# Weight tiles of the FP4 feed-forward dealt over the attention sweeps by a table instead of one per head pair

## The chip, the cores and the metric

The kernel runs on the 8 cores of one Trainium2 chip, each core on one batch element (4096 tokens of 1024 channels) with the same program and no exchange between cores. The metric is the device time in microseconds (us) of the slowest core.

## The reference

Per batch element, with x of 4096x1024:

```python
xn = layernorm(x)
# causal attention, 16 heads of 64, one shared k and v head, then an output layernorm
q = layernorm(xn) @ w_q.T ; k, v = split(layernorm(xn) @ w_kv.T)
s = layernorm(softmax(causal(q k^T)) v @ w_out.T)
# FP4 feed-forward: blocks of 16 along the contracted axis, grid 0 .5 1 1.5 2 3 4 6
def fp4_linear(x, w): return fp4_quant_dequant(x) @ fp4_quant_dequant(w).T
h = silu(fp4_linear(xn, w_gate)) * fp4_linear(xn, w_up)    # w_gate, w_up: 2816x1024
g = silu(fp4_linear(h, w_down))                            # w_down: 1024x2816
out = x + s * g
```

All three feed-forward weights have to be quantized and transposed before the feed-forward begins. That is 52 tiles of 128 rows: 22 of w_gate and 22 of w_up with 1024 columns (short tiles), and 8 of w_down with 2816 columns (long tiles).

## The kernel before

The kernel has three stages. `emit_w` transposes the attention weights. `emit_a` (L586) does the attention, the preparation of x and, in between, the 52 weight tiles. `emit_f` does the feed-forward from DRAM copies of the quantized, transposed weights, behind a barrier on everything before it.

`emit_a` has nine turns of `sup` (0 to 8). Turn 0 prepares four row tiles of x. Each turn from 1 to 8 runs `emit_sweeps(sup - 1)`: 512 queries against 4·sup key tiles, for eight head pairs `w` (0 to 7). After it come the output projection with its layernorm, and `emit_qhat` for the next 512 queries. I call one head pair of one turn a slot; there are 64. A slot of turn `sup` has 4·sup keys: for each key TensorE writes scores to `ps_a` or `ps_b`, ScalarE takes the exponential into `expb`, TensorE accumulates in `ps_o`. At the end ScalarE copies `ps_o` to `aosb`, forms the reciprocal row sums `rb`, sends them through DRAM (`dsw_d`, back as `dtsw`), and VectorE multiplies them in (`AOn`, L547).

Ahead of the sweep of slot w a closure `inject[w]` (L635) emits other work. In turns 1 to 7 it prepares the four next row tiles of x: `p0_ve_part` (L320, layernorm, quantization and a second layernorm on VectorE, with two small ScalarE instructions in each `ln_apply`) in w0 to w3, and `p0_pe_part` (L338, transposes, key and value projections) one slot later, in w1 to w4. Then, in every slot, it emits the weight work:

- `w_tile_pe` (L296) for the tile pending from the slot before: for each 128 columns a TensorE transpose of `wcast` into `ps_o` and a VectorE copy to `xqTst`, in groups of up to eight, each group followed by a store issued from ScalarE's queue. A group waits (L301) until the store before has landed.
- `w_tile_ve` (L282) for the next tile: its load to `wtile` on SyncE's queue, which waits until the tile before is quantized, and `quant` on VectorE, in pieces of 1024 columns, into `wcast`. The tile becomes pending.

So each slot takes one tile. The tiles are used up in order: turns 1 to 5 have the first 40 short tiles, turn 6 has the last four short ones in w0 to w3 and long ones in w4 to w7, turn 7 has long ones in w0 to w3 with the last transposes in w4, and turn 8 has none. The `while` loop at L642 would take what is left, and finds nothing.

Every engine runs its instructions in the order in which this program emits them. A wait in `transpose_chunks` (L194) stands in TensorE's own stream, ahead of the score matmuls of the slot, and the copies stand in VectorE's stream behind `AOn` of the slot before:

```python
        pe.wait(ve, pe_gate_ve)          # L194: the quantized tile
        ...
            npt = pe.op("transpose", tgt[:, 0:128], src_ap[:, sl(ch)],
                        s["identb"][:])
            ve.wait(pe, npt)
            self._tr_free[ch % 2] = ve.op("tensor_copy", dst_fn(ch),
```

`wcast` has two buffers, `wtile` one, the staging buffer of `xqTst` for weights one.

Of the kernel before, what the change touches and what calls it, by code (L numbers as in the profile page):

```python
# [78 lines left out]
class Builder:  # L79
# [506 lines left out]
    def emit_a(self):  # L586
        pe, ve, ac, po, ld, stq = (self.pe, self.ve, self.ac, self.po,
                                   self.ld, self.stq)
        s, st_ = self.s, self.streams
        NSUP = self.NSUP  # L590

        ve.wait_dma(st_["Lmisc"], self._n_greps)
        ve.wait_dma(st_["Swsp"], st_["Swsp"].n)
        self.xt_free = [0, 0]
        self.xst_free = [0, 0]
        self.sst_free = [0, 0]
        self._vtr_free = 0
        self._k2_evac = 0
        self._k2r_ac = 0
        self._op_free_ve = 0  # L600
        self._xqt_pe = [0, 0]
        self._xnlt_pe = [0, 0]
        self._pe_after_sweeps = 0
        self._preA_ve = 0
        self._ao_free = (ve, 0)
        self.aosb_free_ve = [0, 0]
        self.nmd = 0
        self.nmq = 0
        self.n_k2 = 0

        for sup in range(NSUP + 1):
            if sup == 0:
                for t in range(4):
                    nx = self.p0_ve_part(t)
                    self.p0_pe_part(t, nx)
            if sup >= 1:
                base = 4 * sup
                nx_hold = {}

                def mk_both(ttv, ttp, _b=base, _h=nx_hold, _last=(sup == NSUP)):  # L620
                    def f():
                        if not _last:
                            if ttv is not None:
                                _h[ttv] = self.p0_ve_part(_b + ttv)
                            if ttp is not None:
                                self.p0_pe_part(_b + ttp, _h[ttp])
                        if self._w_pend is not None:
                            self._w_tile_pe(self._w_pend)
                            self._w_pend = None
                        if self.wffn_parts:  # L630
                            self._w_pend = self._w_tile_ve(
                                *self.wffn_parts.pop(0))
                    return f

                inject = [mk_both(0, None), mk_both(1, 0),  # L635
                          mk_both(2, 1), mk_both(3, 2),
                          mk_both(None, 3), mk_both(None, None),
                          mk_both(None, None), mk_both(None, None)]
                self.emit_sweeps(sup - 1, inject)
            if sup < NSUP:  # L640
                self.emit_qhat(sup)
        while self.wffn_parts or self._w_pend is not None:  # L642
            if self._w_pend is not None:
                self._w_tile_pe(self._w_pend)
                self._w_pend = None
            if self.wffn_parts:
                self._w_pend = self._w_tile_ve(*self.wffn_parts.pop(0))
# [340 lines left out]
```

How the kernel before makes its waits and increments, by code:

```python
    def wait(self, other, val):  # L35
        if val > 0:
            self.e.wait_ge(other.sem, val)
# [1 line left out]
    def wait_dma(self, dmaq, n):  # L39
        if n > 0:
            self.e.wait_ge(dmaq.sem, 16 * n)
# [1 line left out]
    def op(self, name, *a, **k):  # L43
        if self.serialize and self.n > 0:
            self.e.wait_ge(self.sem, self.n)
        r = getattr(self.e, name)(*a, **k)
        r.then_inc(self.sem, 1)
        self.n += 1
        return self.n
# [7 lines left out]
    def wait(self, other, val):  # L57
        if val > 0:
            self.e.wait_ge(other.sem, val)
# [1 line left out]
    def wait_dma(self, stream, n):  # L61
        if n > 0:
            self.e.wait_ge(stream.sem, 16 * n)
# [9 lines left out]
    def dma(self, out, in_, **k):  # L73
        self.q.e.dma_start(out=out, in_=in_, **k).then_inc(self.sem, 16)
        self.n += 1
        return self.n
# [572 lines left out]
    def emit_f(self):  # L649
# [147 lines left out]
                po.op("tensor_tensor", s["t0f"][:], s["t0f"][:], s["g_sb"][:],  # L797
                      ALU.mult)
                sld_free[fb] = po.n
                po.wait_dma(st_["So%d" % fb], o_free[fb])
                no = po.op("tensor_tensor", s["o_sb"][:, fb, :], s["t0f"][:],
                           s["xr"][:, fb, :], ALU.add)
                xr_free[fb] = no
                stq.wait(po, no)
                o_free[fb] = st_["So%d" % fb].dma(g["out_d"][sl(gt), :],
                                                  s["o_sb"][:, fb, :])
        self.nc.sync.wait_ge(st_["So0"].sem, 16 * st_["So0"].n)
        self.nc.sync.wait_ge(st_["So1"].sem, 16 * st_["So1"].n)
```

## Time and profile before

| | |
|---|---|
| median of 2 runs | 7600.37 us (7597.98 to 7602.76) |
| profiled execution | 7599.55 us, span of its slowest core 7598.0 us |
| spans of the 8 cores | 7546.9 to 7598.0 us |
| busy on the slowest core | DVE 55%, PE 48%, ACT 25% |
| attention stage | to about 4970 us, the feed-forward from there |

PE is TensorE's matmuls, DVE is VectorE, ACT is ScalarE, SP is SyncE. A "q" behind an engine's name is its own instruction stream, from which DMAs are issued. The clock is TensorE's granted clock as a share of 2.4 GHz. All times in the trace are microseconds from the start of the span of core 4, the slowest. Every instruction has the line of the helper that issues it (L46), so groups are told apart by the tiles that they write and read.

### The profile page before, as it was taken

The numbers are of one execution on the slowest core, as the hardware profiler recorded it, in microseconds if no ns is written. First come the engines' busy times: TensorE is split into PE (matmuls) and PEld (weight loads), VectorE is DVE, ScalarE is ACT, GpSimd is POOL, SyncE is SP. The second block draws the span as 40 slices with busy tenths as digits, with TensorE's granted clock in tenths as the row PEclk, the third lists the DMA queues.
The fourth block names the chain that finished last, engine by engine and source line by source line (L and its number), as shares of the span: only waits on it lengthen the run. The fifth ranks groups of instructions, "written<-read, shape, count | busy, mean of one in ns | idle before, by whom it ended". The sixth has DMA issues, their size and how long they took to land.

```text
span 7598.0 us, 56896 instructions; the slowest of 8 cores (7546.9 to 7598.0 us)
## 1 busy us (share of the span) xinstructions
PE 3646.3 (48%) x12721; PEld 1345.8 (18%) x12952; DVE 4146.2 (55%) x6907; ACT 1905.8 (25%) x2394; POOL 194.7 (3%) x119
## 2 busy tenths in 40 slices
PE   2224243344354455435444657644565565546556
PEld 1011011111111111111111212211221122122112
DVE  5575663653553543447477110058838846883883
ACT  0112222232242343334232637601101100100110
POOL 0000000000000000000000000000020010002002
PEclk9756566666666677667666879867777777768777
DMA  2011010110100000011001000020020002002001
GB/s 72 17 32 31 27 36 21 32 32 16 31 25 21 24 27 23 19 32 36 24 31 36 17 9 12 13 79 23 14 81 23 25 31 61 23 14 80 26 22 47
DMA packets 210741, 236.14 MB, mean 31 GB/s; under 512 B 110696, under 2 KB 159976, under 8 KB 209256
## 3 DMA queue, kind: packets, MB, share of 16 engines
q1 hardware_dynamic: 88992, 164.78, 6.9%
q10 hardware_dynamic: 121424, 67.72, 3.1%
q8 instruction: 120, 1.97, 0.1%
q14 instruction: 205, 1.68, 0.1%
HBM read 164.76 MB, written 67.70 MB: 31 GB/s over the span
## 4 chain that ended last, share of the span: by engine, by line
DVE 43%; PE 23%; ACT 12%; issue 11%; DMA 7%; DVEq 2%; ACTq 1%; SPq 1%; POOL 0%; POOLq 0%
DVE f_qs_c L46 16%; PE ps_o L46 14%; DVE qs_c L46 8%; PE ps_a L46 6%; ACT expb L46 6%; PE ps_b L46 3%; DVE f_qs_m L46 3%; DVE t0f L46 2%; DVE bn L46 2%; DVE hq L46 2%; DVE hsb L46 2%; DMA dsw_d<-rb 2%; DMA dtsw<-dsw_d 2%; DVEq L45 1%; DVE qs_m L46 1%
## 5 line engine op out<-in xcount | busy, mean ns | idle before, releaser
L46 PE MATMUL ps_o<-expb,VhX 128*128 128x512 bf16 x2213 | 744.9, 417 | 314.8 <-ACT expb L46 278.7
L46 PE MATMUL ps_a<-wgb,xqT_S 128*128 128x512 bf16 (+1 forms) x1475 | 742.8, 504 | 101.3 <-DMA wub<-wquT_s 77.0
L46 ACT ACTIVATE expb<-ps_a 128x1024 bf16<-128x1024 f32 x576 | 589.3, 1023 | 798.2 <-PE ps_a L46 714.9
L46 PE MATMUL ps_b<-wub,xqT_S 128*128 128x512 bf16 (+1 forms) x1536 | 761.1, 496 | 10.3 <-issue 5.3
L46 DVE TENSOR_TENSOR AOn<-aosb,dtsw 64x512 bf16<-64x512 f32 x128 | 87.9, 686 | 1149.9 <-DMA dtsw<-dsw_d 1142.6
L46 DVE SCALAR_TENSOR_TENSOR f_qs_c<-f_qs_aa,f_qs_c 128x512 f32<-128x512 f32 (+1 forms) x960 | 621.6, 648 | 104.1 <-DVE f_qs_c L46 5.5
L46 DVE SCALAR_TENSOR_TENSOR qs_c<-qs_aa,qs_c 128x1024 f32<-128x1024 f32 (+1 forms) x500 | 601.8, 1204 | 53.1 <-DVE qs_c L46 1.4
L46 ACT ACTIVATE expb<-ps_b 128x1024 bf16<-128x1024 f32 x576 | 589.3, 1023 | 152.1 <-PE ps_b L46 122.7
L46 PE MATMUL ps_a<-identb,hq 128*128 128x128 bf16 x704 | 104.8, 298 | 1037.4 <-DVE hq L46 1037.4
L46 PE MATMUL ps_o<-identb,xq_t 128*128 128x128 bf16 x256 | 60.1, 255 | 1072.4 <-DVE xqTst L46 953.6
L46 PE MATMUL ps_o<-identb,wcast 128*128 128x128 bf16 x664 | 169.2, 264 | 685.4 <-DVE xqTst L46 414.0
L46 PE MATMUL ps_a<-QT,KT 65*128 65x512 bf16 x1152 | 433.2, 444 | 33.3 <-DMA QT<-mrow_d 31.8
L46 PE MATMUL ps_b<-QT,KT 65*128 65x512 bf16 x1152 | 420.0, 432 | 0.7 <-issue 0.4
L46 ACT ACTIVATE lnv<-st,epsT 128x1 f32<-128x1 f32 x96 | 28.3, 294 | 1413.6 <-DVE st L46 1413.6
L46 PE MATMUL ps_o<-wqd_sb,hqT 128*128 128x512 bf16 x1376 | 350.2, 417 | 45.8 <-ACT g_sb L46 38.4
L46 ACT ACTIVATE hqT<-ps_a 128x512 bf16<-128x512 bf16 (+1 forms) x192 | 107.8, 561 | 1025.8 <-PE ps_a L46 1025.8
L46 DVE TENSOR_TENSOR hsb<-hg,ps_b 128x512 f32<-128x512 f32 (+1 forms) x192 | 123.4, 643 | 411.3 <-ACT hg L46 391.8
L46 ACT ACTIVATE hg<-ps_a 128x512 f32<-128x512 f32 (+1 forms) x192 | 107.8, 561 | 932.5 <-PE ps_b L46 702.0
L46 PE MATMUL ps_o<-w_oT,AOn 128*128 128x512 bf16 x502 | 195.0, 570 | 275.2 <-DVE st_s L46 171.7
L46 PEld LDWEIGHTS ps_o<-expb,VhX 128*128 128x128 bf16 x2304 | 173.0, 101 | 846.3 <-issue 833.2
L46 DVE COPY xqTst<-ps_o 128x128 bf16<-128x128 bf16 x784 | 176.0, 224 | 183.3 <-PE ps_o L46 88.6
L46 PEld LDWEIGHTS ps_a<-wgb,xqT_S 128*128 128x128 bf16 x1536 | 199.5, 130 | 414.8 <-issue 358.8
(107 smaller groups left out, 4767.0 us busy)
## 6 DMA issues: line engine op xcount, KB each, us to landing
wgb<-wqgT_s SPq DMA_DIRECT2D x20, 1024.0 KB, 6.0
wub<-wquT_s SPq DMA_DIRECT2D x20, 1024.0 KB, 8.4
x_t<-L_attn_x SPq DMA_DIRECT2D x32, 512.0 KB, 4.5
dsw_d<-rb ACTq DMA_DIRECT2D x128, 128.0 KB, 2.4
dtsw<-dsw_d SPq DMA_DIRECT2D x128, 128.0 KB, 2.6
xr<-L_attn_x SPq DMA_DIRECT2D x32, 512.0 KB, 4.9
out<-o_sb ACTq DMA_DIRECT2D x32, 512.0 KB, 4.9
wtile<-L_ffn_w_gate SPq DMA_DIRECT2D x22, 512.0 KB, 4.2
```

The lines of the kernel that those rows point to most:

```text
L45: self.e.wait_ge(self.sem, self.n)
L46: r = getattr(self.e, name)(*a, **k)
```

## The change

A table `wq` says how many weight tiles a turn takes, and `nsl` spreads them over its eight slots; the weight part of the closure is repeated so often. With eight sweeps the table is: turns 1 to 4 none, turn 5 one tile per slot (8), turn 6 two per slot (16), turn 7 two per slot (16), turn 8 twelve, in the slots w0 to w7 as 1, 2, 1, 2, 1, 2, 1, 2. That is 52. The x preparation stays where it was. In a slot with two tiles the order of emission is: transposes and copies of the pending tile, load and quantization of a first tile, transposes and copies of that first tile, load and quantization of a second tile, which is then pending. In a turn with no tiles the loop body of the weight part doesn't run, so nothing pending is handled either. The 52nd tile is pending when turn 8 ends, and its transposes fall to the `while` loop at L642.

In order, turns 5 to 7 and the first four tiles of turn 8 are the short tiles (40 and 4), and the last eight of turn 8 (from the first tile of w3 on) are the long ones.

```diff
             if sup >= 1:
                 base = 4 * sup
                 nx_hold = {}
+                wq = {NSUP - 3: 8, NSUP - 2: 16,
+                      NSUP - 1: 16, NSUP: 12}.get(sup, 0) if NSUP >= 4 else 7
 
-                def mk_both(ttv, ttp, _b=base, _h=nx_hold, _last=(sup == NSUP)):
+                def mk_both(ttv, ttp, nw, _b=base, _h=nx_hold,
+                            _last=(sup == NSUP)):
                     def f():
                         if not _last:
                             if ttv is not None:
                                 _h[ttv] = self.p0_ve_part(_b + ttv)
                             if ttp is not None:
                                 self.p0_pe_part(_b + ttp, _h[ttp])
-                        if self._w_pend is not None:
-                            self._w_tile_pe(self._w_pend)
-                            self._w_pend = None
-                        if self.wffn_parts:
-                            self._w_pend = self._w_tile_ve(
-                                *self.wffn_parts.pop(0))
+                        for _ in range(nw):
+                            if self._w_pend is not None:
+                                self._w_tile_pe(self._w_pend)
+                                self._w_pend = None
+                            if self.wffn_parts:
+                                self._w_pend = self._w_tile_ve(
+                                    *self.wffn_parts.pop(0))
                     return f
 
-                inject = [mk_both(0, None), mk_both(1, 0),
-                          mk_both(2, 1), mk_both(3, 2),
-                          mk_both(None, 3), mk_both(None, None),
-                          mk_both(None, None), mk_both(None, None)]
+                def nsl(i):
+                    return wq * (i + 1) // 8 - wq * i // 8
+
+                inject = [mk_both(0, None, nsl(0)), mk_both(1, 0, nsl(1)),
+                          mk_both(2, 1, nsl(2)), mk_both(3, 2, nsl(3)),
+                          mk_both(None, 3, nsl(4)), mk_both(None, None, nsl(5)),
+                          mk_both(None, None, nsl(6)),
+                          mk_both(None, None, nsl(7))]
                 self.emit_sweeps(sup - 1, inject)
```

## Rows read from the trace of the kernel before

**Rows 1.** The page: its first line, and the chain that ended last, by engine.
```profile
span 7598.0 us, 56896 instructions; the slowest of 8 cores (7546.9 to 7598.0 us)
...
DVE 43%; PE 23%; ACT 12%; issue 11%; DMA 7%; DVEq 2%; ACTq 1%; SPq 1%; POOL 0%; POOLq 0%
```

**Rows 2.** Waits of PE: engine tile <- releaser: us in total, times, longest us.
```profile
PE ps_o L46 <- DVE xqTst L46: 1375.6, 347, 41.2
...
PE ps_o L46 <- DVE wcast L46: 128.6, 26, 15.9
```

**Rows 3.** Timeline of turn 1, w5 to w6: start us, us, what, [idle before <- releaser].
```profile
608.62 1.29 ACT L46 ACTIVATE aosb<-ps_o 128x512 f32<-128x512 f32 x2 [1.30 <-PE ps_o L46]
...
617.03 0.39 PE L46 MATMUL ps_o<-identb,wcast 128*128 128x128 bf16 x2 [8.98 <-DVE wcast L46]
618.59 1.48 DVE L46 TENSOR_TENSOR AOn<-aosb,dtsw 64x512 bf16<-64x512 f32 x2 [1.81 <-DMA dtsw<-dsw_d]
620.17 0.55 DVE L46 COPY xqTst<-ps_o 128x128 bf16<-128x128 bf16 x2
...
622.62 0.59 PE L46 MATMUL ps_a<-QT,KT 65*128 65x512 bf16 x1
...
623.26 1.22 DVE L46 TENSOR_REDUCE qs_m<-wtile 128x64 f32<-128x1024 f32 x1
...
639.05 1.23 DVE L46 TENSOR_TENSOR wcast<-qs_c,qs_d 128x1024 bf16<-128x1024 f32 x1
```

**Rows 4.** Windows: stretch, us, busy of PE, PEld, DVE, ACT, POOL, clock, DMA, GB/s.
```profile
4228.20:4267.00 38.80, 32.79 (x120) 10.89 (x123) 0.31 (x2) 28.64 (x28) 0.00 (x0) 0.90 0.02 6
...
4309.00:4351.40 42.40, 32.22 (x120) 10.68 (x121) 1.37 (x2) 31.71 (x34) 0.00 (x0) 0.88 0.05 13
...
4571.30:4901.90 330.60, 251.84 (x932) 82.90 (x949) 9.61 (x14) 250.67 (x259) 0.00 (x0) 0.91 0.04 12
```

**Rows 5.** Timeline of ACT, turn 7, w4 to w5 (no tile in w5).
```profile
4267.03 1.29 ACT L46 ACTIVATE aosb<-ps_o 128x512 f32<-128x512 f32 x2 [1.00 <-PE ps_a L46]
...
4271.94 1.02 ACT L46 ACTIVATE expb<-ps_a 128x1024 bf16<-128x1024 f32 x1 [1.46 <-issue]
...
4275.28 1.02 ACT L46 ACTIVATE expb<-ps_a 128x1024 bf16<-128x1024 f32 x1 [1.21 <-PE ps_a L46]
4276.99 1.02 ACT L46 ACTIVATE expb<-ps_b 128x1024 bf16<-128x1024 f32 x1 [0.68 <-PE ps_b L46]
```

**Rows 6.** Timeline of PE in the same stretch.
```profile
4273.21 1.01 PE L46 MATMUL ps_o<-expb,VhX 128*128 128x512 bf16 x2 [5.58 <-ACT expb L46]
```

**Rows 7.** Timeline of turn 5, w1 to w2, with x preparation and one short tile.
```profile
2601.99 1.48 DVE L46 TENSOR_TENSOR AOn<-aosb,dtsw 64x512 bf16<-64x512 f32 x2 [23.00 <-DMA dtsw<-dsw_d]
...
2641.16 0.27 PE L46 MATMUL ps_o<-identb,wcast 128*128 128x128 bf16 x1
...
2644.50 1.01 PE L46 MATMUL ps_a<-QT,KT 65*128 65x512 bf16 x2
```

**Rows 8.** Timeline of turn 2, w0.
```profile
814.76 0.20 ACT L46 ACTIVATE rstd<-lnv 128x1 f32<-128x1 f32 x1
...
822.60 1.02 ACT L46 ACTIVATE expb<-ps_a 128x1024 bf16<-128x1024 f32 x1 [7.63 <-PE ps_a L46]
```

**Rows 9.** Timelines of DVE, ACT and PE, turn 6, w5 to w6, with long tiles.
```profile
3483.11 0.55 DVE L46 COPY xqTst<-ps_o 128x128 bf16<-128x128 bf16 x2
...
3498.01 1.22 DVE L46 TENSOR_REDUCE qs_m<-wtile 128x64 f32<-128x1024 f32 x1
...
3546.18 1.48 DVE L46 TENSOR_TENSOR AOn<-aosb,dtsw 64x512 bf16<-64x512 f32 x2
...
3561.49 1.01 PE L46 MATMUL ps_a<-QT,KT 65*128 65x512 bf16 x2
...
3531.44 1.29 ACT L46 ACTIVATE aosb<-ps_o 128x512 f32<-128x512 f32 x2 [1.00 <-PE ps_o L46]
```

**Rows 10.** DMA issues: out<-in, queue, count, KB each, median us to landing.
```profile
wtile<-L_ffn_w_down SPq DMA_DIRECT2D x8, 1408.0 KB, 6.3
```

## The prediction

> **What bounds the kernel now.** I read the page first. The chain that ended last is DVE for 43% and PE for 23% [rows 1], so it changes hands, and an average says little. The list of PE's waits shows where they meet: PE stood 1375.6 us for copies of transposed tiles (`xqTst`) and 128.6 us for a quantized weight tile (`wcast`) [rows 2]. To see what a slot (one head pair of one turn) pays I then read three kinds of it in the timeline, and their lengths in the windows.
>
> A slot with one short tile and no x preparation [rows 3]: the sweep ends at 608.62 (`aosb`). The tile was quantized before 617.03, but its copies stand on DVE behind `AOn`, which waits for the round trip of the row sums through DRAM and starts at 618.59. The copies run from 620.17, PE reaches the next scores at 622.62, 14.0 us after `aosb`; over the 15 such slots of turns 1 to 5 this gap is 14.0 to 15.3, mean 14.4. Then DVE quantizes the next tile from 623.26 to 640.28 (17.0 us) beside the sweep. Note what sets the 14 us: the round trip (10.0) and `AOn` (1.6), and only the last 3.1 us are the copies. The quantization costs nothing, it lies under sweep and round trip. Coupling PE to DVE is the price, and it is paid once per slot, whatever is quantized beside the sweep.
>
> A slot with no tile [rows 5]: from `aosb` at 4267.03 to the next exponential at 4271.94, 4.9 us, because PE emits the next scores at once and `AOn` is nobody's business. In lengths at 28 keys [rows 4]: 38.8 from first score to `aosb`, plus 14.4 is 53.2 with a tile; 42.4, 42.0 and 42.1 without (the first stands in the rows). **A coupled slot costs 11.0 us more than a free one.** In turn 8 the seven slots w1 to w7 are free, 330.6/7 = 47.2 us each [rows 4].
>
> A slot with x preparation (w1 to w3; w4 has its TensorE half) is coupled anyway: `AOn` at 2601.99, then the preparation on DVE and its own copies; the weight tile's transposes begin only at 2641.16 and the scores at 2644.50 [rows 7]. So there a short tile costs 3.3 us.
>
> **The change, part by part.** Five prices are needed.
>
> 1. A coupling added or taken away: 11.0 us.
> 2. A short tile's copies in a slot that is coupled anyway: 3.3 us.
> 3. A second short tile in a slot. Its transposes wait for its own quantization, and they stand in PE's stream ahead of the sweep. Nothing lies beside it: DVE comes from the pending tile's copies, PE and ACT have nothing else before the scores. 17.1 us of quantization (pitch from one piece of 1024 to the next; the single one above was 17.0), 0.6 us until the first transposed pair is ready to copy (an estimate: two transposes of 0.27 [rows 7]), 3.1 us of copies (620.17 to 623.26 [rows 3]): 20.8 us. The trace never shows a tile quantized and transposed in one slot, so this sum has bounds: not below 17.0 + 3.1 = 20.1, since both are DVE's own work in order, and not above 20.8 plus a load that comes late. The load of the first tile waits for nothing in that slot (the pending tile was quantized in the slot before). The load of the second tile waits for the first's quantization and has the copies to hide in, and what is left lies under the sweep. I take 20.8.
> 4. A second long tile: its quantization takes 3498.01 to 3546.18, 48.2 us, its copies with the two waits for staging stores 3483.11 to 3498.01, 14.9 us [rows 9]. With 0.5 us of start, 63.6. Its load lands 6.3 us after issue [rows 10], and it is issued behind the `dtsw` loads, some 8 us after `aosb`, where DVE wants it 14.4 us after: nothing, or 2 us in one slot.
> 5. A long pending tile instead of a short one: 14.9 - 3.1 = 11.8 us. In turn 6 the long quantization also outlasted the sweep: `aosb` 3531.44, `AOn` 3546.18, 14.7 instead of 10, scores at 3561.49, a gap of 30.0 [rows 9]. In turn 8, 43.9 us of sweep and 10.1 of round trip cover 48.2.
>
> Also w0: there PE isn't held by x preparation (nothing precedes), but ACT is, by the second `rstd` of `ln_apply`, which stands in ACT's stream ahead of the exponentials. In turn 2 it ends at 814.96, and the first exponential runs at 822.60, after the tile's copies and the scores [rows 8]. Without a pending tile the scores are ready long before, and the exponential would start some 0.1 us behind the `rstd`: 7.5 us gained, in turns 2 to 5.
>
> Gains:
> - turn 1: w1 to w4 4 x 3.3, w5 to w7 3 x 11.0: 46.2
> - turns 2 to 4: the same and 7.5 for w0, 53.7 each: 161.1
> - turn 5: w0 only, since it still has a tile per slot: 7.5
>
> Together 214.8 us.
>
> Losses:
> - turn 6 (was: short in w0 to w3, long quantized from w4): w0 to w4 5 x 20.8 = 104.0. w5 to w7: gap 14.4 + 20.8 = 35.2 instead of about 30.1: 3 x 5.1 = 15.3. Sum 119.3.
> - turn 7 (was: long pending in w0 to w4, w5 to w7 free): w0 20.8 - 11.8, less 5.3 for an `AOn` of turn 6 that is no longer late: 3.7. w1 to w4: 4 x (20.8 - 11.8) = 36.0. w5 to w7: 3 x (11.0 + 20.8) = 95.4. Sum 135.1.
> - turn 8 (was free): w0 has one pending short tile behind the wait for `QT` (L463 stands ahead of `inject`), 3.3. w1: 31.8. w2: 11.0. w3, a second long tile behind a short pending one: 11.0 + 63.6 = 74.6. w4, one long pending: 22.8. w5: 22.8 + 63.6 = 86.4. w6: 22.8. w7: 86.4. Sum 339.1.
> - the tail: the last long tile's transposes after the last output projection, with nothing beside them and the feed-forward's barrier behind: 14.9, and 0.6 for a store that lands later than the last of `s_s`. 15.5.
>
> Together 609.0 us. Net **+394.2 us**. The feed-forward isn't touched.
>
> The profiled execution took 7599.55 us (span 7598.0), 0.8 us under the median of the runs. 7599.6 + 394.2 = 7993.8, so I say 7994 us, 5.2% longer.
>
> One place where the clock could move the gains. With a tile, PE comes to each sweep out of a long idle time; a free sweep too finds PE idle, since it waits 5.58 us for the first exponential and its first pair of matmuls takes 1.01 us [rows 6], the same as the first scores of a coupled one (1.01 [rows 7]). The clock over a whole sweep of 28 keys is 0.90 coupled and 0.88 free [rows 4]. So I let free and coupled sweeps cost the same per key. The Trainium skill (TensorE: Matmul & The Clock Gate, "HAM oscillation — how this bites in real kernels") says that waits between bursts of matmuls drop the clock to half again and again, and that a loop that keeps PE busy keeps it up. By that rule the 12 freed sweeps of turns 1 to 4 would open at the full clock and save the 1.21 + 0.68 = 1.9 us for which ACT waits on slow scores at a sweep's start [rows 5], some 22 us more gain, and the sum would be 372 instead of 394. The rows speak against it: that wait stands in a free sweep.
>
> **The rivals.**
>
> *A, the forecast:* the second tile holds PE. 7994 us. Chance 0.86.
>
> *B, the other side: the second tile's work is hidden.* DVE idles some 23 us in a slot before `AOn` ([rows 7], "23.00 <-DMA dtsw<-dsw_d"), so there is room, and it would take DVE running the quantization there. The change adds 17 first short tiles and 3 long ones. If all of their price vanished, 17 x 20.8 + 3 x 63.6 = 544.4 us go from the sum: 7449 us, 2.0% faster. If only quantization vanished and the copies stayed, 435 us go: 7559 us, no change. It turns to faster by over 2% only where 546 us or more vanish. Against it: in the order of emission the first tile's quantization comes behind the pending tile's copies, these behind `AOn`, and the wait of PE's transposes is ahead of the scores. Chances: 0.01 for faster, 0.03 for no change.
>
> *C: the early turns give back little.* If freed slots of 4 to 16 keys were still paced by the round trip of the row sums (`aosb` waits for the `dsw_d` store before, and this for the `dtsw` load before that), only the 3.1 us of copies would go in those 12 slots: 12 x 7.9 = 95 us less gain, 8089 us. For it: the trace has no free slot under 28 keys. Against: the round trip of 10 us fits into the shortest free slot, which is 4.9 + 4 x 1.7 = 11.7 us at the slow opening pace of 1.71 us per key [rows 5]. Chance 0.05.
>
> *D: the late sweeps slow down.* If after 35 to 90 us of idle time PE stayed at the lower of its two clocks (1.2 GHz), a key would take the 1.71 us of a sweep's opening [rows 5] instead of 1.3 (36.5 us over 28 keys), over 8 x (24 + 28 + 32) keys 270 us: 8264 us. Against it: the sweep behind a gap of 37 us has a mean clock of 0.90 [rows 4]. Chance 0.05.
>
> **How the numbers follow.** Own errors of A: a start of a second tile 1 us off either way, 20 us; w0 not gained, 30 us more; the freed sweeps with or without the 22 us; loads late by 2 us in a few slots. That makes 7945 to 8045. The range goes a little beyond, 7930 to 8065, toward C at the upper end, and holds about 0.83. Two per cent (152 us) is about what a measurement of this kernel tells from no change. A, C and D are slower by more: 0.96. The same 0.03, faster 0.01.
>
> **What would show it.** Right: in turns 1 to 4 PE's gap from `aosb` to the scores in w5 to w7 falls from 14 to 0, and the turns end some 50 us earlier each; in turn 8 the slots take 47 + 32, + 11, + 75, + 23, + 86, + 23, + 86 us; PE's wait for `wcast` grows from 129 us to over 450, and the transposes of the first tiles wait 17 or 48 us each; the feed-forward takes its 2628 us as before (4970 to 7598). Wrong: first scores of a two-tile slot under 20 us after the end of the pending tile's copies, or exponentials of a sweep while a first tile is being quantized (B); free early slots that last over 15 us at 4 keys and 20 at 8 (C); over 1.35 us per key in turns 7 and 8 (D).

## Result and the profile after

| | before | after |
|---|---|---|
| median | 7576.95 us (8 runs, 7566.34 to 7602.76) | 7965.17 us (9 runs, 7951.46 to 7992.6) |
| profiled execution, slowest core | 7598.0 us | 7960.2 us |

The changed kernel is slower: ratio 1.0512, 95% interval 1.0493 to 1.053. The medians are 388.2 us apart; the prediction's sum was +394.2. The predicted 7994 us stands 29 us above the median of the changed kernel, because the sum was made against the profiled execution of before (7599.6 us), which is 23 us above the median that more runs gave. The rest is 6 us. The measured time lies inside the stated range of 7930 to 8065 us.

The page of the changed kernel says little by itself: the same instructions (56896), the same busy time of DVE, a chain with nearly the same shares as [rows 1].

```profile
span 7960.2 us, 56896 instructions; the slowest of 8 cores (7923.2 to 7960.2 us)
...
PE 3618.4 (45%) x12721; PEld 1341.2 (17%) x12952; DVE 4148.1 (52%) x6907; ACT 1905.7 (24%) x2394; POOL 194.7 (2%) x119
...
DVE 42%; PE 24%; ACT 12%; issue 11%; DMA 7%; DVEq 2%; ACTq 1%; SPq 1%; POOL 0%; POOLq 0%
```

The waits of PE (engine tile <- releaser: us, times, longest) are where it shows. They answer [rows 2]: what PE stands for quantized weight tiles grew from 128.6 to 520.5 us, with a longest wait of 49.2 us, the quantization of one long tile.

```profile
PE ps_o L46 <- DVE xqTst L46: 1291.1, 346, 40.9
...
PE ps_o L46 <- DVE wcast L46: 520.5, 41, 49.2
```

From the `aosb` of a turn's last slot to that of the next turn's, on the slowest core of each profile (core 4 before, core 2 after; in us, worked out from the `aosb` rows of the timelines):

| turn | before | after | difference | predicted |
|---|---|---|---|---|
| 1 | 655.7 | 607.8 | -47.9 | -46.2 |
| 2 | 514.6 | 458.6 | -56.0 | -53.7 |
| 3 | 551.5 | 498.8 | -52.7 | -53.7 |
| 4 | 591.8 | 532.4 | -59.4 | -53.7 |
| 5 | 629.0 | 621.1 | -7.9 | -7.5 |
| 6 | 716.9 | 835.3 | +118.4 | +119.3 |
| 7 | 734.0 | 873.8 | +139.8 | +135.1 |
| 8 | 508.4 | 847.8 | +339.4 | +339.1 |

Both gains and losses stand where the sum had put them. One core against one other is a rough comparison, though. Each core against itself, the eight attention stages grew by 349 to 379 us, in the mean 364, where the eight turns of the prediction add up to 379: turns 1 to 8 changed by -51.1, -55.8, -55.4, -58.0, -8.1, +117.0, +137.8 and +337.6 us. So the gains came out 14 us larger than forecast and the losses of turns 6 to 8 1 us smaller, and that the medians agree with the sum to 6 us is in part luck. With the tail (14 us) the mean start of the feed-forward moved by 378; what the remaining 10 us of the 388 are isn't told by these two profiles.

What the early turns give back, slot by slot, is in the windows of the changed kernel (stretch, us, busy of the engines, clock, DMA, GB/s): w5 of turn 1, w6 of turns 2, 3 and 4, without a tile, then w7 of turn 7 with two short ones, and w3 and w7 of turn 8 with two tiles each.

```profile
566.50:580.10 13.60, 8.34 (x25) 2.78 (x24) 1.37 (x2) 7.13 (x9) 0.00 (x0) 0.75 0.15 40
1029.60:1047.20 17.60, 11.11 (x40) 3.85 (x40) 1.37 (x2) 11.22 (x13) 0.00 (x0) 0.81 0.11 30
1518.30:1541.80 23.50, 16.20 (x56) 5.53 (x56) 1.37 (x2) 15.32 (x17) 0.00 (x0) 0.78 0.09 23
2042.30:2070.00 27.70, 19.39 (x72) 6.59 (x72) 1.37 (x2) 19.45 (x21) 0.00 (x0) 0.88 0.07 20
4353.40:4427.80 74.40, 36.92 (x132) 12.23 (x134) 35.87 (x50) 31.68 (x33) 0.00 (x0) 0.72 0.10 29
4744.50:4867.50 123.00, 43.45 (x161) 14.72 (x164) 89.04 (x122) 35.77 (x37) 0.00 (x0) 0.65 0.12 36
5141.00:5275.60 134.60, 48.48 (x177) 16.65 (x180) 98.11 (x144) 35.82 (x37) 0.00 (x0) 0.63 0.12 37
```

The first line is 13.6 us where the slot had 23.4 to 23.7 before. The last is 134.6 us where turn 8 had 47.2 [rows 4], and PE is busy 48.5 of them.

A second short tile, turn 6, w5 (timelines of DVE and PE; start, us, what, [idle before <- releaser]). It answers [rows 3]: there the quantization lay beside a sweep, here PE and ACT do nothing while DVE quantizes, from 3361.26 until the transposes at 3378.53.

```profile
3361.26 1.22 DVE L46 TENSOR_REDUCE qs_m<-wtile 128x64 f32<-128x1024 f32 x1
...
3377.05 1.23 DVE L46 TENSOR_TENSOR wcast<-qs_c,qs_d 128x1024 bf16<-128x1024 f32 x1
3378.53 0.39 PE L46 MATMUL ps_o<-identb,wcast 128*128 128x128 bf16 x2 [17.78 <-DVE wcast L46]
3378.97 0.55 DVE L46 COPY xqTst<-ps_o 128x128 bf16<-128x128 bf16 x2 [0.69 <-PE ps_o L46]
...
3381.42 1.01 PE L46 MATMUL ps_a<-QT,KT 65*128 65x512 bf16 x2
```

And a second long tile, turn 8, w5: PE waits 48.84 us, for the whole quantization of that tile, before it can issue one transpose, and the scores come 14.7 us behind that.

```profile
5012.47 0.39 PE L46 MATMUL ps_o<-identb,wcast 128*128 128x128 bf16 x2 [48.84 <-DVE wcast L46]
...
5027.12 1.01 PE L46 MATMUL ps_a<-QT,KT 65*128 65x512 bf16 x2
```

### The profile page after: what moved, and what is told of

It is laid out like the page before. It is cut to its first block, busy times and chain, and to the rows that moved or that the text cites. A ratio compares the mean times of both kernels' runs of the same rounds, so it can differ in the third digit from the quotient of the medians.

```text
span 7960.2 us, 56896 instructions; the slowest of 8 cores (7923.2 to 7960.2 us)
## 1 busy us (share of the span) xinstructions
PE 3618.4 (45%) x12721; PEld 1341.2 (17%) x12952; DVE 4148.1 (52%) x6907; ACT 1905.7 (24%) x2394; POOL 194.7 (2%) x119
## 4 chain that ended last, share of the span: by engine, by line
DVE 42%; PE 24%; ACT 12%; issue 11%; DMA 7%; DVEq 2%; ACTq 1%; SPq 1%; POOL 0%; POOLq 0%
DVE f_qs_c L46 15%; PE ps_o L46 14%; DVE qs_c L46 8%; ACT expb L46 6%; PE ps_a L46 6%; PE ps_b L46 4%; DVE f_qs_m L46 3%; DMA dtsw<-dsw_d 2%; DVE t0f L46 2%; DVE bn L46 2%; DVE hq L46 2%; DMA dsw_d<-rb 2%; DVE hsb L46 2%; DVE qs_m L46 2%; ACT rb L46 2%
## 5 line engine op out<-in xcount | busy, mean ns | idle before, releaser
L46 PE MATMUL ps_o<-identb,wcast 128*128 128x128 bf16 x664 | 166.7, 263 | 945.9 <-DVE wcast L46 520.5
L46 PE MATMUL ps_o<-wqd_sb,hqT 128*128 128x512 bf16 x1376 | 318.4, 389 | 45.1 <-ACT g_sb L46 38.5
```

Source lines behind the costliest of these rows:

```text
L46: r = getattr(self.e, name)(*a, **k)
```

## The experiments

The theory, A: a tile has a price because its transposes stand in PE's stream ahead of a sweep, behind `AOn` of the slot before and (for a slot's first of two tiles) behind their own quantization. The quantization itself is free as long as it lies beside a sweep. The main rival: VectorE is the engine with most work, so its work is the price, and late turns simply got too much of it. Each kernel was timed against the kernel before on the same chip.

### e1: no tile is transposed in the slot of its quantization

```diff
-                        for _ in range(nw):
-                            if self._w_pend is not None:
-                                self._w_tile_pe(self._w_pend)
-                                self._w_pend = None
-                            if self.wffn_parts:
-                                self._w_pend = self._w_tile_ve(
-                                    *self.wffn_parts.pop(0))
+                        while self._w_pend:
+                            self._w_tile_pe(self._w_pend.pop(0))
+                        for _ in range(nw):
+                            if self.wffn_parts:
+                                self._w_pend.append(self._w_tile_ve(
+                                    *self.wffn_parts.pop(0)))
```

> The changed kernel with the same table, but no tile is transposed in the slot in which it is quantized: all pending tiles (up to two) are transposed first, then the slot's tiles are quantized. Theory A (PE waits for a first tile's own quantization ahead of the sweep): 17 short first tiles give back 20.9 us each and cost 3.2 us of copies in the next slot, so 300 us go in turns 6 and 7 and in w1 of turn 8; two long tiles (2 x 48.2 us and a load of 6.3 us between them) outlast sweep and round trip (54 us) by some 49 us, so the long slots give back 63.6 and pay 49 + 14.9, nothing in sum. 7965 - 300 = 7665 us, 1.012 of before. Rival (the late turns simply have too much VectorE work, wherever PE waits): as the changed kernel, 7965 us.

Measured: 7722.14 us (median of 4), ratio to before 1.0194 (1.0163 to 1.0225). Same table and same VectorE work in the same turns, and 241 to 243 us of the 388 are gone (ratios, medians), so the rival falls. The expectation was missed by 57 us. The trace names most of it: two pending tiles use one staging buffer, so between them DVE waits for the first one's store (timeline of DVE, turn 6, w5 to w6).

```profile
3324.85 1.48 DVE L46 TENSOR_TENSOR AOn<-aosb,dtsw 64x512 bf16<-64x512 f32 x2 [5.28 <-DMA dtsw<-dsw_d]
...
3328.86 0.56 DVE L46 COPY xqTst<-ps_o 128x128 bf16<-128x128 bf16 x2 [0.26 <-PE ps_o L46]
3332.60 0.55 DVE L46 COPY xqTst<-ps_o 128x128 bf16<-128x128 bf16 x2 [3.19 <-DMA wqgT_s<-xqTst]
```

In the whole run DVE waits for such a store in the 17 slots that begin with two pending short tiles, 54.4 us in sum (DVE's waits; w_gate's and w_up's tiles), where the changed kernel has none of these waits:

```profile
DVE xqTst L46 <- DMA wquT_s<-xqTst: 31.8, 10, 3.2
DVE xqTst L46 <- DMA wqgT_s<-xqTst: 22.6, 7, 3.5
```

So the second tile's copies cost 6.2 us (gaps of 20.2 to 21.0 instead of 14.3) and not 3.2. In turn 8 the long tiles did as expected: `aosb` of w3 at 4548.93, its `AOn` at 4609.63, 60.7 us later instead of 10, because two long quantizations outlast the sweep. The gain there was given back as a late round trip.

### e2 and e3: the quantization of the weight tiles left out, before and after

```diff
-                self.quant(s["wtile"][:, off:off + w],
-                           s["wcast"][:, wslot, off:off + w], w,
-                           v_dma=(st_["Lwt"], nl))
+                ve.wait_dma(st_["Lwt"], nl)
+                ve.op("tensor_copy", s["wcast"][:, wslot, off:off + w],
+                      s["wtile"][:, off:off + w])
```

> The kernel before with the quantization of the 52 weight tiles left out: a plain copy to bf16 stands in its place (0.7 us per 1024 columns instead of 17.1), all transposes, waits, loads and stores stay. Theory A (what a tile costs is the coupling of PE to VectorE once per slot, the quantization is hidden): only what outlasted the sweep goes, 19 us in turn 6, 5 in turn 7, some 5 elsewhere: 7577 - 29 = 7548 us, 0.996. Rival (VectorE's time is the price, as its 43% of the chain suggests): 60 x 16.3 + 8 x 13 = 1082 us of VectorE work go, and at 43% of them 465 us: 7110 us or less.

Measured: 7549.32 us (median of 10), ratio 0.997 (0.9955 to 0.9985). First lines of its page, beside DVE's 4146.2 us of the kernel before:

```profile
span 7572.7 us, 55087 instructions; the slowest of 8 cores (7513.7 to 7572.7 us)
...
PE 3712.3 (49%) x12952; PEld 1347.5 (18%) x12952; DVE 3169.7 (42%) x5887; ACT 1908.7 (25%) x2394; POOL 195.0 (3%) x119
```

976 us of work were taken from the engine with the largest share of busy time and of the chain, and the kernel became 0.3% faster. This is the clearest number of the study: in the kernel before, the quantization of weights is hidden almost wholly. The expectation was 7548 us, the rival's 7110 or less, so the rival falls.

> The changed kernel with the same quantization left out (a plain copy to bf16 instead). Theory A: 17 short first tiles give back 16.4 us each (279) and 3 long ones 46 each (138), and a few us of late round trips: 7965 - 420 = 7545 us, as much as the kernel before without quantization. Rival (the double tiles cost by their copies, stores and waits, not by the quantization): above 7850 us. Second rival (all VectorE work counts alike): as much less as in the kernel before.

Measured: 7574.09 us (median of 10), ratio 1.001 (0.9993 to 1.0027). The same edit that took 16 to 23 us from the kernel before (medians, ratio) takes 380 to 391 from the changed one, and the two kernels then differ by 0.4%. So nearly the whole net loss is exposed quantization, as the sum had it. Both rivals fall: it isn't above 7850 us, and the effect is not the same in both kernels. PE's waits agree: for `wcast` it now stands 74.7 us (520.5 in the changed kernel). The time missed 7545 by 29 us, and the trace shows why. DVE now waits 47.3 us for staging stores of short tiles, in 18 places. The changed kernel has none of these waits, because there the quantization between two tiles' copies covers the store.

```profile
PE ps_o L46 <- DVE wcast L46: 74.7, 37, 15.9
...
DVE xqTst L46 <- DMA wquT_s<-xqTst: 24.8, 10, 2.8
DVE xqTst L46 <- DMA wqgT_s<-xqTst: 22.5, 8, 3.1
```

### e4: a wait without a tile

```diff
                 inject[w]()
+            if sup < 4 and w >= 5:
+                pe.wait(ve, ve.n)
```

> The changed kernel, and in w5 to w7 of turns 1 to 4, which have no tile, PE waits before the sweep for the last VectorE instruction emitted (the multiplication by the row sums of the slot before). No work is added. Theory A (coupling is the price of a slot): from aosb to the first exponential 13.1 us (10.0 round trip, 1.6 AOn, 1.5 scores) instead of 4.9, 12 x 8.2 = 98 us: 8063 us, 1.064 of before. Rival (a slot pays for the tile's transposes and copies, the wait alone costs nothing): 7965 us.

Measured: 8050.4 us (median of 4), ratio 1.063 (1.0597 to 1.0662): 1.18 points over the changed kernel, 89 us in 12 slots, where 98 had been expected and the rival said none. In the profiles the attention stage is 97 us longer than in the changed kernel (mean of the eight cores), 96 of it in turns 1 to 4, so the 9 us that the medians fall short lie outside those slots. Timelines of ACT and PE, turn 2, w5 to w6:

```profile
1060.68 1.28 ACT L46 ACTIVATE aosb<-ps_o 128x512 f32<-128x512 f32 x2 [1.00 <-PE ps_o L46]
...
1073.64 1.02 ACT L46 ACTIVATE expb<-ps_a 128x1024 bf16<-128x1024 f32 x1 [9.52 <-PE ps_a L46]
...
1072.42 1.01 PE L46 MATMUL ps_a<-QT,KT 65*128 65x512 bf16 x2 [12.01 <-DVE AOn L46]
```

From `aosb` to the next exponential 13.0 us, against 4.9 in the changed kernel without the wait:

```profile
1029.56 1.29 ACT L46 ACTIVATE aosb<-ps_o 128x512 f32<-128x512 f32 x2 [1.00 <-PE ps_a L46]
...
1034.46 1.02 ACT L46 ACTIVATE expb<-ps_a 128x1024 bf16<-128x1024 f32 x1 [1.46 <-issue]
```

One wait, with no work behind it, costs 8.1 us of the 11.0 that a coupled slot pays. The remaining 3 are about what the copies take (3.1 us [rows 3]); no run leaves out the copies alone.

### e5: the transposes inside the sweep

If the place of the transposes is the whole price, they can be put where nobody waits: two per key, inside a sweep, once `AOn` of the slot before is done. This kernel is built from the one before. The core of its edit, in the loop over keys of `emit_sweeps` (the rest of the edit, new helpers for pieces and a table of slots, is left out, and the two comments are added here):

```diff
                 self._sim_free_ac[k % 2] = nex
                 pend = (k, nex, 0)
+                if late and k >= late[0][0]:
+                    late.pop(0)[1]()              # store to DRAM, two keys later
+                if kst is not None and (k >= kst or not steps):
+                    if steps:
+                        for _ in range(2):
+                            if steps and steps[0] is not None:
+                                steps.pop(0)()    # one transpose and its copy
+                        if steps and steps[0] is None:
+                            steps.pop(0)
+                            late.append((k + 2, stores.pop(0)))
+                    if not steps:
+                        while nw > 0:
+                            self._w_quant()
+                            nw -= 1
```

> Built from the kernel before, all tiles computed as there. The pending tile's transposes are no longer ahead of a sweep but inside it, two per key, from key 1 in slots with x preparation and from key 6 in the others (by then AOn of the slot before is done); the slot's own tile is quantized behind them. w_down is taken in pieces of 1024, 1024 and 768 columns, so there are 68 pieces; wtile and the staging buffer have two halves. Dealt as 4 pieces in turns 1 and 2 (w0 to w3, transposes ahead as before), 8 in turns 3 to 6, 12 in turn 7, 16 in turn 8. Theory A (a tile costs only because its transposes stand ahead of the sweep, behind AOn): turns 3 to 8 take what turns without tiles take: 499 and 532 us as in the changed kernel, then 42 us more for each four keys (575, 617, 658) and 508 for turn 8; turns 1 and 2 621 and 472. Sum 4482 instead of 4902, and 8 us of tail: 7577 - 412 = 7165 us, 0.946. Up to 2 us per slot more if the transposes disturb the sweep: 7260. Rival 1 (the copies lengthen a sweep as they lengthen a gap, 3.2 us a piece): 7380. Rival 2 (the change's price is VectorE work in the late turns): slower than before, since turn 8 now has 16 pieces where it had none.

Measured: 7186.07 us (median of 4), ratio 0.9472 (0.944 to 0.9504). It beats both kernels, with all tiles computed and DVE as busy as before:

```profile
span 7196.2 us, 57174 instructions; the slowest of 8 cores (7134.0 to 7196.2 us)
...
PE 3619.7 (50%) x12952; PEld 1336.1 (19%) x12952; DVE 4148.5 (58%) x6907; ACT 1907.3 (27%) x2394; POOL 194.7 (3%) x119
```

Its turns 3 to 8 took 503, 541, 575, 612, 656 and 514 us, where 499, 532, 575, 617, 658 and 508 were expected; turns 1 and 2 took 626 and 479 instead of 621 and 472. Turn 8 has 16 pieces in it and is 334 us shorter than in the changed kernel, which has twelve tiles (28 pieces) there. One of its sweeps (timeline of PE, w7 of turn 8): the first transposes come 15.6 us after `aosb`, then a pair with each key in between the matmuls, and none of these rows of PE has a wait.

```profile
4473.07 0.28 PE L46 MATMUL ps_o<-identb,wcast 128*128 128x128 bf16 x2
4473.19 0.60 PE L46 MATMUL ps_b<-QT,KT 65*128 65x512 bf16 x2
4473.82 0.59 PE L46 MATMUL ps_o<-expb,VhX 128*128 128x512 bf16 x2
4474.25 0.49 PE L46 MATMUL ps_o<-identb,wcast 128*128 128x128 bf16 x2
4474.66 0.59 PE L46 MATMUL ps_a<-QT,KT 65*128 65x512 bf16 x2
```

The slot before it in a window: 47.8 us, as against 47.2 with no tile [rows 4], and DVE is busy 34 of them.

```profile
4409.70:4457.50 47.80, 37.52 (x154) 12.85 (x153) 34.38 (x52) 35.86 (x38) 0.00 (x0) 0.89 0.16 42
```

### e6: the same, with the transposes ahead of the sweep again

e5 changed three things: where the transposes stand, how tiles are cut and dealt, and the second buffers. This one takes back the first alone. The stores, and the instructions that quantize the slot's own pieces, are emitted behind the transposes in both kernels, so they move ahead of the sweep with them.

```diff
             nw, kst = wplan[w]
+            kst = None
```

> The kernel of e5 (68 pieces, two halves of wtile and of the staging buffer, its dealing with 16 pieces in turn 8), with one thing undone: all transposes stand ahead of the sweep again, in every turn. Theory A: turns 3 to 6 get back 7.5 + 4 x 3.3 + 3 x 11.0 = 53.7 us each, turn 7 66.5 (two pending in w1 to w4), turn 8 3.3 + 7 x (11.0 + 3.2) = 102.7, in sum 384, less some 20 us by which the sweeps of e5 were longer than sweeps without tiles: 7186 + 364 = 7550 us, 0.997 of before. Rival (e5 gained by its dealing, its pieces or its second buffers): 7186 us, 0.947.

Measured: 7513.47 us (median of 4), ratio 0.9924 (0.9906 to 0.9941). So of the 5.3% that e5 gains, 4.5 points are the place of the transposes and 0.8 the pieces, the dealing and the buffers together (not told apart further). It came out 37 us below the expectation. A part of that is an error of the sum: it charged 7.5 us for w0 of turn 3, where no piece is pending and nothing changes (178.9 us in e5, 178.7 here). The rest isn't explained. Its slots w1 to w7 of turn 8, with two pieces each, take 59.6 to 61.8 us; the sum had 47.2 + 14.2 = 61.4.

## Why the prediction was right

- **A coupled slot costs 11.0 us more than a free one, whatever is quantized beside the sweep.** Right. In turns 2 to 4, w5 to w7 fell by 10.2 to 12.2 us each, and in turn 1 by 9.4 to 10.0 (a free slot of four keys takes 13.6 to 14.0 us, not the 11.7 used against rival C: all four keys carry the matmuls of the causal mask, and its third and fourth exponentials wait 2.06 and 1.54 us for scores, not 1.21 and 0.68). e4 shows that 8.1 of them are the wait alone, e2 that the quantization has next to no part in it.
- **A tile in a slot with x preparation costs 3.3 us.** A little low: without a tile the gaps of w1 to w4 are 49.1 to 50.2 and 21.8 to 22.3 us, with one 52.9 to 54.5 and 25.7 to 26.0, in the means 4.1 and 3.9 less. For sixteen slots that is some 12 us, the larger part of the 14 us by which the gains were forecast too small.
- **A second short tile costs 20.8 us.** Right: from 3361.26 to the next tile's reduction at 3382.35 it is 21.1, less 0.4 of load wait, which lies under the sweep, 20.7. The estimated start of 0.6 us is the row's 0.69. The gaps of w5 to w7 in turns 6 and 7 are 35.0 to 35.6 (predicted 35.2).
- **A second long tile costs 63.6 us.** Right to 1.3 us: the slots w3, w5, w7 of turn 8 take 123.1, 132.7 and 134.6 us, and the prediction had 47.2 + 74.6 = 121.8, 133.6 and 133.6. w4 and w6, 70.6 and 70.2, had 70.0.
- **w0 gains 7.5 us where no tile is pending, since ACT and not PE is what holds it.** Right: the first exponential starts 0.1 us behind `rstd` in each of turns 2 to 5, where it was 7.6 us before; here turn 2, which answers [rows 8]. The slots got shorter by 8.9, 7.9, 6.7 and 4.8 us.

```profile
764.90 0.20 ACT L46 ACTIVATE rstd<-lnv 128x1 f32<-128x1 f32 x1
765.20 1.02 ACT L46 ACTIVATE expb<-ps_a 128x1024 bf16<-128x1024 f32 x1
```

- **The tail costs 15.5 us.** 14.5: from the end of the last `st_s` to the first load of the feed-forward 16.8 us instead of 2.3.
- **The feed-forward isn't touched.** It took 2628.5 us on the slowest core before and 2602.6 on that of after, but the eight cores spread from 2586.9 to 2628.5 in the one profile and from 2589.3 to 2602.6 in the other. The 26 us lie within that spread (more on it in the last section), and they are why the two profiled spans are only 362 us apart while the start of the feed-forward moved by 388 from the one slowest core to the other.
- **The clock.** The rule of the Trainium skill (TensorE: Matmul & The Clock Gate, "HAM oscillation — how this bites in real kernels") would have let freed sweeps open at full clock. They don't: in the changed kernel's free w6 of turn 2 the third and fourth exponentials again wait 1.21 and 0.68 us for slow scores, as in [rows 5]. The stretch between 1029.60 and 1047.20 has a mean clock of 0.81. PE still idles 5.57 us before the sweep's first `ps_o` matmuls, and these take 1.01 us. So a wait between bursts is still there, and the trace doesn't contradict the page; it was the step from the page to this kernel that didn't hold, and the row decided rightly.

```profile
1035.73 1.01 PE L46 MATMUL ps_o<-expb,VhX 128*128 128x512 bf16 x2 [5.57 <-ACT expb L46]
...
1037.80 1.02 ACT L46 ACTIVATE expb<-ps_a 128x1024 bf16<-128x1024 f32 x1 [1.21 <-PE ps_a L46]
1039.51 1.02 ACT L46 ACTIVATE expb<-ps_b 128x1024 bf16<-128x1024 f32 x1 [0.68 <-PE ps_b L46]
```

Rivals: B (the second tile hidden) would have needed the quantization ahead of `AOn`; it ran behind the pending tile's copies. C (early turns give little) is refuted by 13.6, 17.6, 23.5 and 27.7 us for free slots of 4, 8, 12 and 16 keys. D (late sweeps slow down) as well: behind gaps of 75 to 91 us the sweeps of turns 7 and 8 keep 1.29 to 1.33 us per key (from the first exponential to the last), as before the change (1.29 to 1.34).

Left open: the x preparation holds PE and ACT in the same way. The longest wait of PE in the changed kernel outside weights, 40.9 us, is for its copies, and the 28 slots that have it open with gaps of 22 to 50 us even without a tile. Moving it into the sweeps as e5 does with weights wasn't tried; its two layernorms put ScalarE instructions in front of the exponentials, so it would need another way to the reciprocal root.

## What to carry to other kernels

Price work on a shared in-order stream by what waits behind it and by what its own wait waits for, and not by its engine's busy share: here 976 us of VectorE work were worth 0.3%, and one wait without work 8 us a slot. Before moving work to where an engine is idle, look at the place in the stream where it will stand; two units ahead of a loop can expose the first in full where one was hidden. A transform that needs a round trip between engines (quantize, transpose, copy) goes one iteration late, and inside the body of the loop rather than ahead of it.

## What the runs showed of the hardware that was not expected

The same feed-forward, with the same instructions and data of the same shape, took from 2586.9 to 2628.5 us on the eight cores of one execution, 1.6% apart. The spread goes with the granted clock. From 4975 to 7540 us the two cores with the longest feed-forward (cores 4 and 5, 2628 and 2617 us) have a mean clock of 0.74, the six others (2587 to 2608 us) 0.75, and DVE is busy 1766 to 1767 us on all eight. The profile of e5 has it more plainly: cores 0 to 3 have 0.72 to 0.73 and take 2588 to 2615 us, cores 4 to 7 have 0.75 to 0.76 and take 2568 to 2590. What sets a core's clock wasn't tested. This spread has a part in which core of a profile is the slowest, and the difference of two profiled spans (362 us) was 26 us off the difference of the medians (388). Comparing the same stage turn by turn, each core with itself, avoids it. The other numbers bring no surprise: 20.7 us for a second tile is what rows of before add up to, and the wait of some 3 us between two uses of a staging buffer is the 2.9 us (median) in which its 256 KB stores land in the trace of before.
